# Pacing the gathers of the two attention layers by TensorE's progress

## The reference, cut to what matters

```python
g = h @ W
s = (g * a_src).sum(-1); d = (g * a_dst).sum(-1)
e = leaky_relu(s[src] + d[dst], 0.2)            # the score lookups
ex = exp(e - segment_max(e, dst)[dst])          # the softmax over a node's incoming edges
alpha = ex / segment_sum(ex, dst)[dst]
out = segment_sum(g[src] * alpha[:, None], dst) # the weighted sums
```

## Time and profile before

| | |
|---|---|
| median of 3 runs | 7929.77 us |
| span of the profiled execution | 7961.8 us |
| TensorE, busy | 3988.6 us (50%) |
| VectorE, busy | 3552.5 us (45%) |
| ScalarE, busy | 1543.9 us (19%) |
| GpSimd, busy | 4190.2 us (53%) |
| DMA | 944.43 MB, mean 119 GB/s |

### The profile page before, as it was taken

How to read it: one execution, slowest core, us unless ns; L and a number is a source line. 1 busy time by engine, 2 the same in 40 slices (tenths; PEclk the granted TensorE clock), 3 DMA queues, 4 the chain that set the end, 5 groups by cost and what they waited for, 6 DMA issues and landing times. The chain is left out here.

```text
span 7961.8 us, 106930 instructions
## 1 busy us (share of the span) xinstructions
PE 3988.6 (50%) x29332; PEld 3225.4 (41%) x29332; DVE 3552.5 (45%) x10985; ACT 1543.9 (19%) x3920; POOL 4190.2 (53%) x4416
## 2 busy tenths in 40 slices
PE   2401645540164442334444458888888585333446
PEld 1301534530154432323444446666666473233334
DVE  3002965530297442423333355555555693122224
ACT  0001730010174000200000033444344213000003
POOL 6474035537503566466665635555555644666662
PEclk8655557775555766655555578888888797566568
DMA  5233445643344554345666424445444372111111
GB/s 147 75 105 96 146 125 171 188 117 106 94 145 131 161 168 140 108 104 141 149 150 147 109 87 143 147 149 149 145 147 145 79 206 64 46 46 45 45 45 32
DMA packets 564740, 944.43 MB, mean 119 GB/s; under 512 B 122022, under 2 KB 226111, under 8 KB 563599
## 3 DMA queue, kind: packets, MB, share of 16 engines
q1 hardware_dynamic: 263779, 403.40, 15.9%
q0 software_dynamic: 140576, 316.92, 15.5%
q10 hardware_dynamic: 159840, 217.27, 9.7%
HBM read 703.64 MB, written 235.53 MB: 118 GB/s over the span
## 5 line engine op out<-in xcount | busy, mean ns | idle before, releaser
L256 POOL DMA_INDIRECT s_rows<-rel_tab,src_v x832 | 813.4, 978 | 700.0 <-DVE s_msg L2489 424.7
L256 POOL DMA_INDIRECT stash<-gat_tab,src_g x784 | 790.9, 1009 | 724.5 <-POOLq L111 383.2
L256 POOL DMA_INDIRECT stash<-in_x,src_g x736 | 740.4, 1006 | 719.3 <-POOLq L111 382.6
L1163 PE MATMUL g_psc<-g_parts,g_oh 128*128 128x52 bf16 x9408 | 507.0, 220 | 1060.3 <-issue 796.5
L256 POOL DMA_INDIRECT gcn_rows<-gcn_tab,src_g x784 | 753.0, 960 | 461.8 <-issue 222.4
L256 POOL DMA_INDIRECT ggn_rows<-ggn_tab,src_g x784 | 744.2, 949 | 423.0 <-issue 231.0
L1600 PE MATMUL e_psb<-tmp,e_oh 128*128 x3328 | 565.5, 334 | 751.4 <-DVE e_oh L1571 470.4
L1163 PEld LDWEIGHTS g_psc<-g_parts,g_oh 128*128 128x128 bf16 x9408 | 439.7, 120 | 1128.2 <-issue 843.8
L1600 PEld LDWEIGHTS e_psb<-tmp,e_oh 128*128 128x128 f32 x3328 | 510.5, 237 | 806.7 <-issue 806.5
L1946 PE MATMUL ggn_pso<-ggn_rows,ggn_oh 128*128 x1952 | 448.7, 390 | 652.3 <-issue 277.2
L2116 PE MATMUL gcn_pso<-gcn_rows,gcn_oh 128*128 x1952 | 503.3, 433 | 531.4 <-issue 387.1
(11 more groups left out here) (503 smaller groups left out, 8232.0 us busy)
## 6 DMA issues: line engine op xcount, KB each, us to landing
edge_v<-stash SPq DMA_DIRECT2D x392, 256.0 KB, 2.1
g_lo_rows<-lo_rows ACTq DMA_DIRECT2D x392, 256.0 KB
e_values<-edge_v SPq DMA_DIRECT2D x392, 256.0 KB
oh_dram<-tmp ACTq DMA_DIRECT2D x208, 256.0 KB
s_oh<-oh_dram SPq DMA_DIRECT2D x208, 256.0 KB
edge_v<-acc SPq DMA_DIRECT2D x208, 256.0 KB
r_values<-edge_v SPq DMA_DIRECT2D x208, 256.0 KB, 3.0
tmp<-drel_rows ACTq DMA_DIRECT2D x208, 128.0 KB
```

Of the source, the lines that this page charges most:

```text
L256: pool.indirect_dma_start(rows[:, t, :], None, tab[:, :], bass.IndirectOffsetOnAxis(ap=edges[:, t:t + 1], axis=0)).then_inc(s_land, 16)
L1163: m = nc.tensor.matmul(ps_c[k % 2][:, a * GT + t, 0:NBP], oh[:, k, a * GE + t * P:a * GE + (t + 1) * P], part[:, a, n, :], start=(n == 0), ...
```

## The change

`keep_gathers` gets a semaphore and a function of j. Before gathered group j GpSimd now waits until TensorE's counter has reached that value, ahead of the wait for the buffer. In the score lookups the counter is `s_c` (4 plus the groups done) and the value `RING + (j - 2) * 196 // n` for j above 2, with n = 79 or 76 gathered groups. In the weighted sums it is `s_o` (4 per iteration) and the value `4 * (j * 180 // n)`, with n = 70 or 110. The softmax's gathers are as they were.

```diff
-        def keep_gathers(pool, tab, first, n, s_land, s_st):
+        def keep_gathers(pool, tab, first, n, s_land, s_st, s_pace=None, pace=None):
 
             for j in range(n):
                 r, k = j // KEEP, j % KEEP
+                if s_pace is not None and pace(j) > 0:
+                    pool.wait_ge(s_pace, pace(j))
                 if r > 0:
                     pool.wait_ge(s_st[k], r * 16)
...
+                def lookups(j):
+
+                    return RING + (j - 2) * GROUPS // (last - first) if j > 2 else 0
...
-                        keep_gathers(pool, gat_src(l), first, last - first, k_land, k_st)
+                        keep_gathers(pool, gat_src(l), first, last - first, k_land, k_st, s_c, lookups)
...
+            def added(j):
+
+                return GT * (j * (ITERS - 28) // live)
...
-                        keep_gathers(pool, gat_src(l), first, live, k_land, k_st)
+                        keep_gathers(pool, gat_src(l), first, live, k_land, k_st, s_o, added)
```

## The result

| | before | after |
|---|---|---|
| median | 7934.11 us (4 runs, 7909.9 to 7955.14) | 7475.73 us (4 runs, 7461.38 to 7480.83) |
| ratio after / before | | 0.9421, 95% interval 0.9405 to 0.9438 |
| span of the profiled execution | 7961.8 us | 7479.0 us |

The changed kernel is 5.8% faster, 25 us from the forecast of 7450.

The account below looks back on a forecast made before the run. In the lookups TensorE issues slowly beside GpSimd's unbroken gathers, so the two halves run one after the other. Lookups -442 and sums -20 and -15 make -477: 7485 from the profile, 7450 at the median, range 7180 to 7770 us.

Parts of the forecast that it names:

- The sum: Whole kernel: lookups -442, sums -20 and -15, together -477 us, from the profiled 7961.8 to 7485, forecast as 7450.
- The lookups, 7.0 us a gathered group: Both layers' score lookups: paced gathers cost 7.0 us per group, giving 573 us against 791 and 552 against 776.
- The cycle behind the 7.0: Lookups: GpSimd runs two or three groups, then pauses for TensorE; 13.6 us for two, 23.1 for three.
- crawl: TensorE's slow issue beside unbroken gathers: 67 us a group against 1.84, starting about 8 us in, ending 2 to 3 behind.
- The sums: Weighted sums: fewer gathers at the start let TensorE go faster; 20 us less in the first layer, 15 in the second.
- The waits at nothing: GpSimd's 327 new wait instructions: taken as costing nothing, with 47 us over both lookups kept in the range.
- The rule on VectorE's lock: Lookups: gathers moved beside a busy VectorE are locked out of descriptor writing, 45 us worse, partly in the 7.0 already.
- GpSimd as the bound: Rival for the lookups: the wait breaks runs enough, 5.2 us a gathered group, 7170 us in all; chance 0.18.
- 9 us a group and more: Rival for the lookups: the crawl returns at once after a short pause, 9 us a group, 7760 us; chance 0.17.
- a long recovery: Rival for the lookups: TensorE recovers slowly after each run, with a 12 us tail some 8165 us; chance 0.06.
- The 7 us tail: Argument against slow recovery: after some 100 us of nearly unbroken gathers the crawl ended 7 us later.
- nothing happens: Rival: the crawl is a fixed price of 5.3 us per gather wherever issued, so 7930 us, within 0.5%; chance 0.04.

Follow-up runs that it names:

- e9: The whole change unaltered, run again against the kernel before at the upper level: 7478.42 us beside 7923.3, ratio 0.9426.
- e1: The changed kernel with the wait in the lookups alone, none in the sums, against the kernel before: 5993.42 us beside 5993.08, ratio 1.0003.
- e11: The whole change unaltered, run again against the kernel before at the lower level: 6010.14 us beside 5999.22, ratio 1.0018.

## Why the prediction was right, by its own steps

**The sum.** -477 was forecast from the profiled execution, -483 came. At the median it is 7476 for 7450: the runs' median lies 3 us under the profile (7479.0, 7475.73), where I had taken 32 off. That the sum fits within 6 us is in part luck: the lookups won 7 us less than forecast, the sums 20 more, and all the rest came out 7 longer.

**The lookups, 7.0 us a gathered group.** Right in its size: 307.6 to 862.7 us for 79 groups is 7.03 us, 1465.0 to 2004.4 for 76 is 7.10. The 20 us behind the last gather were 14.6 and 12.3. The stages came at 570.9 and 552.9 against 573 and 552.

**The cycle behind the 7.0.** Right in its mechanism, a crawl that begins in an unbroken run and ends behind it, but wrong in its sizes. From the convolution I had put the crawl's start about 8 us into a run, and so expected runs of two or three groups, 13.6 us for two. In the first layer 37 of the 60 runs are of one group, and with its pause such a run takes some 6.7 us; the prediction didn't have it. The 16 runs of two take 15.5 us each. Lines of one of them, from the timeline of the kernel after:

```profile
383.37 1.36 POOL L256 DMA_INDIRECT stash<-in_x,src_g  x1 [1.77 <-PE g_psc L1170]
387.82 0.59 DVE L1102 TENSOR_TENSOR g_eq<-g_eq,g_psc 128x416 f32<-128x416 f32 x1 [1.14 <-remote]
389.97 0.94 PE L1170 MATMUL g_psc<-g_parts,g_oh 128*128 128x52 bf16 x15 [1.97 <-issue]
392.60 0.94 POOL L256 DMA_INDIRECT stash<-in_x,src_g  x1 [0.31 <-issue]
394.94 0.20 PE L1170 MATMUL g_psc<-g_parts,g_oh 128*128 128x52 bf16 x1 [1.10 <-issue]
395.04 0.59 DVE L1102 TENSOR_TENSOR g_eq<-g_eq,g_psc 128x416 f32<-128x416 f32 x1 [5.12 <-remote]
399.07 0.94 POOL L256 DMA_INDIRECT stash<-in_x,src_g  x1 [5.53 <-PE g_psc L1170]
```

TensorE makes 15 matmuls in one piece until 7.5 us after the run's start and the other 9 of that group in pieces of 1 to 4; the group is done 1.6 us behind the last gather's end, and the `take` comes 7.2 us after the one before. So the full crawl begins and ends about where the forecast had it (8 us, 2.5 us). But GpSimd goes on only 3.9 us after that group, where I had 1.1 us of work to make up. Of the 80 late `take`s 16 are of this kind and cost 83 us over the ordinary 2.02; the other 64, 3.0 to 4.5 us after the one before, cost 77 and lie in the runs of one group too. That smaller delay, well before 8 us, the prediction didn't have; the timeline further up shows one of 4.4 us. The long cycle was priced too low, the short one was missing, and their mixture came out at 7.0; the 7.0 itself I had taken from the rows of stages already paced, and not from the cycle.

**The sums.** -20 and -15 were forecast, -47 and -8 came. The first 52 us of the first sums hold 192 matmuls for 64, 24 iterations for 8: 16 more, where I had counted 13. Measured from the stage's first matmul, the 129th comes after 36.0 us instead of 69.4 and the 385th after 105.1 instead of 152.4, so 33 us are won at the start and 14 soon after; the 11 us that I had taken back for the gathers moved later don't show. Beside fewer gathers the granted clock of those 52 us rose too, 0.83 for 0.60. The second layer has the looser wait and SyncE's order behind it. Its 129th matmul comes 29 us sooner (45.0, 73.6), but only 8 of them are left at the end of the stage, and in e9 none.

**The waits at nothing.** Right: e1 at the lower level is 1.0003 with 149 new waits in it.

**The rule on VectorE's lock.** The Trainium skill ("DMA: Bandwidth & Descriptors", SWDGE vs HWDGE vs iDMA) has GpSimd's descriptor writing locked out by VectorE's two-port mode, which I had priced at 0.07 us for each moved gather, 45 us in all. The averages hide it: 315.9 / 316 = 1.000 us a gather in the first lookups after, beside a VectorE busy for 66% of the time, against 312.19 / 316 = 0.988 beside an idle one. But the gathers differ by what VectorE does beside them. The 141 that overlap its one-hot operation (`g_oh`, L1089) take 1.069 us on average, 73 of them over 1 us, as the gather at 513.64 in the timeline above. The other 175 take 0.944 and none is over 1 us, whatever else VectorE does. The one-hot operation itself takes 0.431 us beside a gather and 0.344 without. That is 141 x 0.125 = 18 us in the first layer, 0.06 us a gather, and as much in the second: the size of the price was right. In the kernel before, 46 of the 316 gathers took over 1 us too, 41 of them beside no one-hot operation, for a reason that no run shows; so the average hardly moved. In e11 the numbers are 0.982 us (196 gathers) and 0.947. Whether L1089 runs in the two-port mode isn't in the trace, and how much of the 18 us the stage paid, with GpSimd waiting for TensorE for 150 us, isn't shown.

**The rivals.** GpSimd as the bound (5.2 us a group, 7170) is wrong at the upper level and exactly the case at the lower one, 5.1 us a group, where the time is 6010 and not 7170 because the other stages are shorter at that level too. Against 9 us a group and more stand the 7.03 measured, and against a long recovery that no two `take`s are over 7.3 us apart in the first lookups. The 7 us tail that I had put against the latter was misread, though: the matmul of the earlier trace rows waited 14.07 us for VectorE's `e_oh`, not for its own issue, so that row measures no end of a crawl. That nothing happens had 0.04 as a price per gather; it happens, for a reason I didn't list: no crawl at all.

**What the prediction didn't question.** It treated the crawl as a property of the kernel. It is one of the conditions that the kernel ran in. At the level shown the forecast holds; at the other the same change is worth -0.2%. That the result fell in the level of the trace that I had read was luck: of six sets of runs two did.

## What to carry to other kernels

Where one engine's slow issue appears beside another's long runs, take the price of pacing from a stage that is already paced: it held to within 2% here (7.03 and 7.10 for 7.0), while the cycle worked out by itself did not. Tie such a pause to the progress of the engine that suffers rather than to a fixed length: the tied wait gave 5.8% where TensorE crawled and cost 0.2% where it didn't, while the fixed pause cost 5.9% there; what a fixed pause gives where TensorE crawls wasn't measured. And before a large share of a profile is explained by the program, run the unchanged kernel again at another time and on another chip.

## What the runs showed of the hardware

The same program has two levels. The kernel before took 7934 and 7923 us in two sets of runs and 5993, 5998, 5998 and 5999 in four others; the changed one 7476 and 7478, and 6010. It isn't bound to a chip: one chip showed 5998 in one set and 7923 in the next. It isn't the number of kernels run together either, as a set of one kernel had either level. Compared over the changed kernel's two traces (7479.0 and 6005.7 us), the difference of 1473 us lies in nearly every stage that gathers: 75 us before the first lookups (306.4, 231.3), 191 and 172 in the lookups, 60 and 112 in the sums, 898 from the end of the second sums (2806.7, 2231.2) on; the softmaxes alone are longer at the lower level, by 25 and 10 us, as more gathers are left for them. GpSimd's gathers are the same in both, 0.944 and 0.947 us at the median, and so are the DMA bytes. Of the 1936 us between the levels the change gives back 458, a quarter; 898 us of what remains lie in the convolution, the edge attention and the gated unit. What makes TensorE issue slowly beside GpSimd's gathers in one set of runs and not in another is open: nothing in a profile that I read names it.
